# Row-maximum transposes ahead of the projections, and the low parts of Q and K taken by VectorE from PSUM

## The chip, the core and the metric

The kernel runs on one core of a Trainium2 chip. A core has five engines with instruction streams of their own: TensorE (PE in the profile; PEld is its weight load), VectorE (DVE), ScalarE (ACT), GpSimdE (POOL) and SyncE (SP), which here issues every DMA. They meet through semaphores. Matmul results go to PSUM, eight banks of 128 x 512 f32 values; everything else lies in SBUF. The metric is the device time of one execution in microseconds (us), lower being better.

## What is computed

```python
x = L0_attn_x                                    # 16 x 256 x 256, f32
xn = layernorm(x)
# attention, 16 heads of 16, causal, per batch of 256 rows
qkv = (xn @ w_qkv).reshape(b, s, 3, 16, 16)
scores = einsum('bqhd,bkhd->bhqk', q / 4, k); scores = where(causal, scores, NEG)
att = einsum('bhqk,bkhd->bqhd', softmax(scores), v).reshape(b, s, 256) @ w_out
# feed-forward part in fp8
ffn = (gelu(xn8 @ w_gating[0]) * (xn8 @ w_gating[1])) @ w_linear
out = x + att + ffn
```

## The kernel before, in words

The 4096 rows are worked off twice. First come 8 **chunks** of 512 rows: layer norm, transposes, the feed-forward part (gate L705, up L712, down L732), and the residual sum; the transposed normalised rows go to DRAM, split in a rounded high part and a low part. Behind chunk 5 the projections of batch 0 are made, behind chunk 6 the Q and K of batch 1 (`first_batches`).

Then 19 **steps** s = 0 to 18 pipeline the attention of the 16 batches (B = 16; `has(b)` is 0 <= b < 16). Heads are split in two halves c = 0, 1, and the score work of a half in two parts ii = 0, 1. A score call (`scores`, lines L771 to L829) does two jobs together: the maxima pass (mask matmuls L771, scores L792 and L825) of one half and the exponent pass (L809, L829) of an older one. In a full step PE runs, in this order,

- S1: maxima (s,0,0) with exponents (s-2,1,1); then QK: `project_qk` of batch s+1, L744, 12 matmuls to each of the banks `misc[0]` and `misc[1]`;
- S2: maxima (s,0,1) with exponents (s-1,0,0); then TM: two small transposes L857 of the row maxima of (s-1,1); then TV: probabilities times V of (s-2,1), L848;
- S3: maxima (s,1,0) with exponents (s-1,0,1); then V: `project_v` of batch s+1, L751; then OUT: `project_out` of batch s-3, L865;
- S4: maxima (s,1,1) with exponents (s-1,1,0); then TM of (s,0) and TV of (s-1,0).

QK, V, OUT, TM and TV all write one of the two banks of `misc`, and each waits for the reader of what stood there. S1 to S4 use the other six banks.

What the other engines do for it:

- DVE reduces each score result to row maxima (L497 for two banks, L500 for the third); a score call waits at its start for the L497 of the call before it (`max_done`). It also turns each TV result to rows (L507), divides it by the sum (L513, L515), and turns it back (L522).
- ACT copies Q and K out of `misc` twice: L593 rounds to the high part (`qk_part`), L596 copies them raw (`qk_raw`, in `w_raw`). POOL then subtracts (L353): low part = raw - high part. ACT also takes the exponents (L619, L621), negates the transposed maxima (`negate_max`, L610), and copies V (L604), the output (L636) and the attention rows (L630).
- POOL masks the exponents (L368, L372), splits the attention rows (L377) and adds x (L382).
- SP sends the parts of Q and K to the operand `stack` of the scores (`fill_stack`, L240, six DMAs for a batch) and the negated maxima to one row of it (`place_max`, L245). The exponent pass of a half waits for that row (`neg_in`). `place_max(s-1, 1)` stands behind the six DMAs of `fill_stack(s+1)` in SP's queue.

Nothing but this written order and the waits sets when something runs; all engines work in order.

## Time and profile before

| what | value |
|---|---|
| median of 3 runs | 385.46 us (385.41 to 386.12) |
| the profiled execution's own time | 386.55 us |
| its span, first to last instruction | 384.5 us |
| mean granted TensorE clock | 0.983 |
| busy: PE, DVE, ACT, POOL | 354.4 us (92%), 264.0 us (69%), 237.9 us (62%), 198.5 us (52%) |
| DMA | 57.5 MB moved, mean 150 GB/s |

A row of the timeline gives start, duration, engine, line, operation, output and inputs, and a count when like instructions are merged; square brackets hold how long the engine had been idle and who ended that. PE's matmuls overlap, so the time that a group takes is the distance from its start to the start of the next group, not its printed duration. The same goes for DVE and ACT, where the next instruction starts up to 0.1 us before the printed end of the last.

### The profile page before, as it was taken

To read this page: it belongs to the slowest core of one execution; us is meant where nothing else is said; L and a number is where in the kernel's file an instruction comes from. 1 tells how busy PE (TensorE), PEld (TensorE's weight loads), DVE (VectorE), ACT (ScalarE), POOL (GpSimd) and SP (SyncE) were. 2 spreads that over 40 slices of the span, in tenths; PEclk is the share of its full clock that TensorE was granted. 3 is DMA by queue.
4 is the path that set the end of the run, shared out by engine and by line. 5 is a ranking of instruction groups with operands and counts; after the bars stand their busy time and mean duration, and the time that the engine had idled before them with its cause. 6 is when DMAs were issued, how large, how long until landed. Compare 5 with 4: busy or idle time off the path is not lost.

```text
span 384.5 us, 9837 instructions
## 1 busy us (share of the span) xinstructions
PE 354.4 (92%) x3882; PEld 269.8 (70%) x3882; DVE 264.0 (69%) x444; ACT 237.9 (62%) x416; POOL 198.5 (52%) x268
## 2 busy tenths in 40 slices
PE   6698899998999889999999999999999999999882
PEld 6354465447475777778877888888888878886662
DVE  5768788885615565767767777776777677768741
ACT  0885666765664155676676666666757666666761
POOL 2351541234241134576666666865766657656773
PEclk9999999999999799999999999999999999999996
DMA  7985734930718034516436346255274362340001
GB/s 239 352 286 163 221 113 126 243 122 0 263 67 274 0 115 164 192 64 217 150 102 235 111 154 220 90 191 178 75 249 150 101 222 100 124 167 32 31 29 55
DMA packets 45453, 57.52 MB, mean 150 GB/s; under 512 B 2656, under 2 KB 36960, under 8 KB 45408
## 3 DMA queue, kind: packets, MB, share of 16 engines
q1 hardware_dynamic: 45408, 56.90, 45.3%
q8 instruction: 31, 0.51, 0.6%
q14 instruction: 14, 0.11, 0.1%
HBM read 16.78 MB, written 12.58 MB: 76 GB/s over the span
## 4 chain that ended last, share of the span: by engine, by line
PE 69%; DVE 8%; SPq 6%; ACT 5%; POOL 4%; issue 4%; DMA 4%; POOLq 0%; DVEq 0%; ACTq 0%
PE ps L744 11%; PE ps L848 10%; PE ps L732 7%; SPq L240 6%; PE ps L751 5%; PE ps L809 5%; PE ps L865 5%; PE ps L792 5%; PE ps L771 5%; PE ps L712 4%; PE ps L705 4%; DVE act L472 4%; PE ps L825 4%; DMA stack<-neg_max 3%; PE ps L681 2%
## 5 line engine op out<-in xcount | busy, mean ns | idle before, releaser
L497 DVE TENSOR_REDUCE row_max<-ps 128x8 f32<-128x1024 f32 x64 | 78.2, 1222 | 40.1 <-PE ps L792 40.0
L619 ACT ACTIVATE arena<-ps 128x1024 f32<-128x1024 f32 x64 | 65.8, 1028 | 43.2 <-PE ps L809 42.8
L368 POOL TENSOR_SCALAR_AFFINE_SELECT arena<-arena 128x1024 f32<-128x1024 f32 x64 | 55.5, 867 | 37.7 <-ACT arena L619 37.0
L472 DVE TENSOR_TENSOR act<-ps,gate 128x512 fp8e4<-128x512 f32 x64 | 43.1, 686 | 26.2 <-ACT gate L562 18.0
L353 POOL TENSOR_TENSOR qk_part<-w_raw,qk_part 128x512 fp32r<-128x512 f32 x32 | 41.0, 1281 | 33.3 <-ACT w_raw L596 32.4
L744 PE MATMUL ps<-xs,wq_part 128*128 128x256 f32 x384 | 50.2, 286 | 1.4 <-DVE wq_part L463 0.7
L744 PEld LDWEIGHTS ps<-xs,wq_part 128*128 128x128 f32 x384 | 46.9, 188 | 3.8 <-DVE wq_part L463 1.0
L848 PE MATMUL ps<-arena,v_aug 128*32 128x256 f32 (+1 forms) x1024 | 48.2, 329 | 0.6 <-POOL arena L372 0.5
L562 ACT ACTIVATE gate<-ps 128x512 bf16<-128x512 f32 x64 | 37.9, 599 | 17.1 <-PE ps L705 11.0
L500 DVE TENSOR_REDUCE row_max<-ps 128x2 f32<-128x512 f32 x64 | 43.5, 680 | 2.6 <-PE ps L825 2.6
L507 DVE STREAM_TRANSPOSE xn<-ps 128x512 f32<-128x512 f32 x32 | 22.9, 716 | 31.1 <-PE ps L848 31.1
L771 PE MATMUL ps<-above,pick 64*128 64x128 bf16 (+1 forms) x384 | 40.4, 242 | 2.6 <-DVE row_max L497 2.5
L712 PE MATMUL ps<-x,wg 128*128 128x512 fp8e4 x128 | 38.0, 378 | 4.9 <-DVE act L472 4.6
L848 PEld LDWEIGHTS ps<-arena,v_aug 128*32 128x32 f32 x1024 | 28.9, 109 | 18.3 <-issue 7.3
L705 PE MATMUL ps<-x,wg 128*128 128x512 fp8e4 x128 | 38.0, 379 | 2.1 <-ACT gate L562 1.0
L621 ACT ACTIVATE arena<-ps 128x512 f32<-128x512 f32 x64 | 38.3, 598 | 0.0
L809 PE MATMUL ps<-stack 64*128 64x128 f32 (+1 forms) x384 | 33.6, 280 | 4.2 <-DMA stack<-neg_max 2.9
L792 PE MATMUL ps<-stack 63*128 63x128 f32 (+1 forms) x384 | 36.7, 297 | 0.0
L382 POOL TENSOR_TENSOR w_raw<-w_raw,xres 128x512 f32<-128x512 f32 x16 | 20.4, 1273 | 28.9 <-ACT w_raw L636 28.9
L303 POOL TENSOR_SCALAR var_eps<-mean_var 128x4 f32<-128x4 f32 x8 | 2.1, 264 | 58.9 <-DVE mean_var L421 58.9
L809 PEld LDWEIGHTS ps<-stack 64*128 64x128 f32 x384 | 26.7, 187 | 6.5 <-DMA stack<-neg_max 4.7
L825 PE MATMUL ps<-stack 63*128 63x256 f32 x128 | 31.2, 324 | 0.0
(64 smaller groups left out, 626.1 us busy)
## 6 DMA issues: line engine op xcount, KB each, us to landing
stack<-qk_part SPq DMA_DIRECT2D x96, 256.0 KB, 2.9
xt_store<-xt_part SPq DMA_DIRECT2D x16, 512.0 KB, 4.1
xs<-xt_store SPq DMA_DIRECT2D x16, 512.0 KB, 3.9
out_dram<-w_raw SPq DMA_DIRECT2D x16, 256.0 KB, 2.2
xres<-in_L_attn_x_dram SPq DMA_DIRECT2D x7, 512.0 KB, 6.5
arena<-in_L_ffn_w_gating_dram SPq DMA_DIRECT2D x2, 1024.0 KB, 9.0
stack<-spare SPq DMA_DIRECT2D x4, 512.0 KB, 7.1
arena<-in_L_ffn_w_linear_dram SPq DMA_DIRECT2D x1, 1024.0 KB, 13.2
```

What stands on the lines that cost most here:

```text
L368: nc.gpsimd.affine_select(diag, diag, pattern=[[0, 1024 // width], [1, P]], compare_op=ALU.is_ge, fill=0.0, base=0, channel_multiplier=-1) ...
L472: nc.vector.tensor_tensor(act8[:, j, :], up_ps[j % 2][:], gate[:, j % 2, :], ALU.mult, saturate=False).then_inc(act_done, 1)
L497: nc.vector.tensor_reduce(to[:, :, 4 - heads:4], max_ps[:, 0:2, :].rearrange("p e (h k) -> p e h k", k=width), axis=AXIS_X, op=ALU.max).th ...
L619: nc.scalar.activation(arena[:, 3 * c + 2 * ii, :, :], exp_ps[:, 0:2, :], ACT.Exp).then_inc(exp_done, 1)
L705: last = nc.tensor.matmul(gate_ps[j % 2][:], wg8[:, 0, k, j * P:(j + 1) * P], x8[:, k, :], start=(k == 0), stop=(k == KD - 1))
L712: last = nc.tensor.matmul(up_ps[j % 2][:], wg8[:, 1, k, j * P:(j + 1) * P], x8[:, k, :], start=(k == 0), stop=(k == KD - 1))
L744: last = nc.tensor.matmul(misc[:, u, s * S:(s + 1) * S], wq_part[:, a, kt, col:col + P], xs[b % 2][:, z, kt, :], start=(i == 0), stop=(i = ...
L771: nc.tensor.matmul(max_ps[:, bank, :].rearrange("p (h k) -> p h k", k=width)[:, :, first:first + 64], pick[rows, i, :], above[rows, :].uns ...
L792: last = nc.tensor.matmul(max_ps[:, u, i * width:(i + 1) * width], st[rows, 4 * c + 4 - heads + i, 0, ii * P:(ii + 1) * P], st[rows, 4 * c ...
L809: last = nc.tensor.matmul(exp_ps[:, u, i * width:(i + 1) * width], est[rows, 4 * ec + 4 - heads + i, 1, kt * P:(kt + 1) * P], est[rows, 4 ...
L825: last_max = nc.tensor.matmul(max_ps[:, 2, cols], st[rows, 4 * c + i, 0, P:S], st[rows, 4 * c + i, 1, :], start=False, stop=(i == 1), skip ...
L848: last = nc.tensor.matmul(pv_bank(b, c)[32 * i:32 * i + 32, u * S + kt * P:(u + 1) * S], va[:, kt, 2 * (HG * c + i) + u, :], cols, start=( ...
```

## The change

Four things are edited.

- ACT's raw copy (L596), `qk_raw` and POOL's subtraction (L353) are gone. DVE subtracts the high part from the PSUM bank itself, in `split_qk`, which now stands in DVE's order between `normalize_o(s-2, 0)` and `find_max(s, 0, 1)`. Whoever waited for the raw copy (`qk_copied`) waits for this subtraction (`qk_lo`).
- TM of (s-1,1) moves from behind S2 to in front of QK, TM of (s,0) from the end of the step to directly behind S3. Both now write bank 1 of `misc`. The second half of QK (bank 1) waits for the first negation, V (bank 1) for the second.
- OUT now stands in front of V. TV of half 0 writes bank 0 instead of bank 1, except for the last half of all, (15,1), which has bank 1.
- ACT negates in the new order, ahead of the copies of Q and K and behind the exponents of S3; SP's `place_max` calls stand ahead of `fill_stack` and right behind it.

```diff
-            return misc[:, 1 if c == 0 or b == B - 1 else 0, :]
+            return misc[:, 1 if 2 * b + c == 2 * B - 1 else 0, :]
...
 (SP)
-                if s == B:
+                if has(s - 1):
                     place_max(s - 1, 1)
                 if s >= 1 and has(s + 1):
                     fill_stack(s + 1, 0)
                     fill_stack(s + 1, 1)
-                if has(s - 1) and s < B:
-                    place_max(s - 1, 1)
+                if has(s):
+                    place_max(s, 0)
                 if has(s + 3):
                     load_xs(s + 3)
                 if has(s - 3):
                     store_y(s - 3)
-                if has(s):
-                    place_max(s, 0)
...
 (DVE)
+            def split_qk(b, g):
+                dve.wait_ge(qk_hi[g], b + 1)
+                nc.vector.tensor_tensor(qk_part[:, g, QLO:KLO + 1:3, :], misc[:, g, :].rearrange("p (a s) -> p a s", a=2),
+                                        qk_part[:, g, QHI:KLO, :].bitcast(F32), ALU.subtract).then_inc(qk_lo[g], 1)
...
                 if has(s - 2):
                     normalize_o(s - 2, 0)
+                if s >= 1 and has(s + 1):
+                    split_qk(s + 1, 0)
+                    split_qk(s + 1, 1)
                 if has(s):
                     find_max(s, 0, 1)
...
 (ACT)
                 if has(s - 2):
                     exponent(s - 2, 1, 1)
+                if has(s - 1):
+                    negate_max(s - 1, 1)
                 if s >= 1 and has(s + 1):
                     copy_qk(s + 1, 0)
                     copy_qk(s + 1, 1)
...
                     exponent(s - 1, 0, 1)
+                if has(s):
+                    negate_max(s, 0)
+                if has(s - 3):
+                    copy_y(s - 3)
                 if has(s + 1):
                     evacuate_v(s + 1)
...
 (PE)
+                if has(s - 1):
+                    pe.wait_ge(*((v_done, s + 1) if has(s) else (neg_done[0], s)))
+                    transpose_max(s - 1, 1)
                 if s >= 1 and has(s + 1):
-                    pe.wait_ge(neg_done[0], s)
+                    pe.wait_ge(*((o_by_q_done, turned(s - 2, 0)) if s >= 2 else (ffn_done, 2 * CHUNKS)))
                     project_qk(s + 1, 0)
-                    pe.wait_ge(*((o_by_q_done, turned(s - 2, 0)) if s >= 2 else (v_done, 2)))
+                    pe.wait_ge(neg_done[1], s)
                     project_qk(s + 1, 1)
...
                 if has(s - 2) and s <= B:
-                    pe.wait_ge(*((qk_copied[0], s + 2) if has(s + 1) else (neg_done[0], s)))
+                    pe.wait_ge(*((qk_lo[0], s + 2) if has(s + 1) else (o_by_q_done, turned(s - 2, 0))))
                     times_v(s - 2, 1)
...
+                if has(s):
+                    pe.wait_ge(*((ffn_done, 2 * CHUNKS) if s == 0 else (qk_lo[1], s + 2) if has(s + 1) else (neg_done[1], s)))
+                    transpose_max(s, 0)
                 if has(s - 3):
...
                     for c in range(2):
                         project_out(s - 3, c)
+                if has(s + 1):
+                    pe.wait_ge(neg_done[0], s + 1)
+                    project_v(s + 1)
```

Where the order changes, a full step in the middle. **PE, S1 and the projections**, before and after (the first row is the last matmul of S1, the last three begin S2):

```order
L829 MATMUL ps<-stack 128x256
L744 MATMUL ps<-xs,wq_part 128x256 x24
L771 MATMUL ps<-above,pick 128x2x64 x4
L792 MATMUL ps<-stack 128x256 x4
L809 MATMUL ps<-stack 128x128 x8
```

```order
L818 MATMUL ps<-stack 128x256
L846 MATMUL ps<-ident,row_max 8x128 x2
L733 MATMUL ps<-xs,wq_part 128x256 x24
L760 MATMUL ps<-above,pick 128x2x64 x4
L781 MATMUL ps<-stack 128x256 x4
```

The two transposes (L857, now L846) stand in front of the projections (L744, now L733).

**DVE, first half of a step**, before and after, with the semaphores that each row waits for; L507/L499 turns the TV result, L497/L489 and L500/L492 are the maxima:

```order
L522 STREAM_TRANSPOSE xn<-o_norm 128x256 [waits ot_lo,o_norm_done]
L497 TENSOR_REDUCE row_max<-ps 128x2x2 [waits max_ready]
L500 TENSOR_REDUCE row_max<-ps 128x2 [waits max_ready]
L507 STREAM_TRANSPOSE xn<-ps 128x512 [waits pv_ready]
L497 TENSOR_REDUCE row_max<-ps 128x8 [waits max_ready]
```

```order
L514 STREAM_TRANSPOSE xn<-o_norm 128x256 [waits ot_lo,o_norm_done]
L472 TENSOR_TENSOR qk_part<-ps,qk_part 128x2x256 [waits qk_hi0]
L472 TENSOR_TENSOR qk_part<-ps,qk_part 128x2x256 [waits qk_hi1]
L489 TENSOR_REDUCE row_max<-ps 128x2x2 [waits max_ready]
L492 TENSOR_REDUCE row_max<-ps 128x2 [waits max_ready]
L499 STREAM_TRANSPOSE xn<-ps 128x512 [waits pv_ready]
```

The maxima of S2 are now queued behind the two subtractions.

**SP, one step**, before and after; L240/L238 fills the stack, L245/L243 places the maxima, L230/L228 loads `xs`, L250/L248 stores the output:

```order
L240 DMA stack1<-qk_part 32x4x512 [waits exp_ready,qk_lo0]
L240 DMA stack1<-qk_part 32x8x256 x2
L240 DMA stack1<-qk_part 32x4x512 [waits exp_ready,qk_lo1]
L240 DMA stack1<-qk_part 32x8x256 x2
L245 DMA stack3<-neg_max1 2x4x256 [waits neg_done1]
L230 DMA xs1<-xt_store 128x1024 [waits v_ready]
L250 DMA out_0_dram<-w_raw 128x2x256 [waits y_done]
L245 DMA stack0<-neg_max0 2x4x256 [waits neg_done0]
```

```order
L243 DMA stack3<-neg_max1 2x4x256 [waits neg_done1]
L238 DMA stack1<-qk_part 32x4x512 [waits exp_ready,qk_lo0]
L238 DMA stack1<-qk_part 32x8x256 x2
L238 DMA stack1<-qk_part 32x4x512 [waits exp_ready,qk_lo1]
L238 DMA stack1<-qk_part 32x8x256 x2
L243 DMA stack0<-neg_max0 2x4x256 [waits neg_done0]
L228 DMA xs0<-xt_store 128x1024 [waits v_ready]
L248 DMA out_0_dram<-w_raw 128x2x256 [waits y_done]
```

The maxima of half 1 are sent ahead of the six DMAs, those of half 0 ahead of the load and the store.

## Rows read from the trace of the kernel before

**Rows 1.** Timeline of PE, one step without a wait: start us, us, engine, line, what.

```profile
165.18 0.39 PE L771 MATMUL ps<-above,pick 64*128 64x256 bf16 x4
...
166.61 3.14 PE L744 MATMUL ps<-xs,wq_part 128*128 128x256 f32 x24
169.68 0.29 PE L771 MATMUL ps<-above,pick 64*128 64x128 bf16 x4
...
171.00 0.38 PE L857 MATMUL ps<-ident,row_max 128*8 128x128 f32 x2
171.31 1.51 PE L848 MATMUL ps<-arena,v_aug 128*32 128x256 f32 x32
172.75 0.39 PE L771 MATMUL ps<-above,pick 64*128 64x256 bf16 x4
...
174.18 1.68 PE L751 MATMUL ps<-wq_part,xs 128*128 128x256 f32 x12
175.69 1.60 PE L865 MATMUL ps<-wq_part,xt_part 128*128 128x256 f32 x12
177.22 0.28 PE L771 MATMUL ps<-above,pick 64*128 64x128 bf16 x4
...
180.30 0.39 PE L771 MATMUL ps<-above,pick 64*128 64x256 bf16 x4
```

**Rows 2.** Timeline of PE: S1 of step 15.

```profile
348.90 0.39 PE L771 MATMUL ps<-above,pick 64*128 64x256 bf16 x4
```

**Rows 3.** Waits of the whole span: total us, times, longest us.

```profile
PE ps L809 <- DMA stack<-neg_max: 2.9, 5, 0.8
```

**Rows 4.** Chain that ended last, step 14: start us, us, what.

```profile
343.84 0.04 issue
343.89 2.21 DMA stack<-neg_max
```

**Rows 5.** Timeline of ACT in the step of rows 1.

```profile
169.78 0.59 ACT L593 CAST qk_part<-ps 128x512 fp32r<-128x512 f32 x1 [0.36 <-PE ps L744]
...
179.64 0.36 ACT L610 ACTIVATE neg_max<-ps 8x256 fp32r<-8x256 f32 x1
```

**Rows 6.** Timeline of DVE: a subtraction from PSUM (chunk 7), a maximum (step 3).

```profile
107.38 1.29 DVE L439 TENSOR_TENSOR xt_part<-ps,xt_part 128x512 fp32r<-128x512 f32 x2 [1.97 <-ACT xt_part L553]
...
170.30 1.23 DVE L497 TENSOR_REDUCE row_max<-ps 128x4 f32<-128x1024 f32 x1 [1.15 <-PE ps L792]
```

**Rows 7.** Timeline of PE, chunk 7 and steps 0 and 1.

```profile
115.84 0.59 PE L712 MATMUL ps<-x,wg 128*128 128x512 fp8e4 x2 [0.23 <-DVE act L472]
...
128.80 0.61 PE L771 MATMUL ps<-above,pick 64*128 64x256 bf16 x4 [0.73 <-DVE row_max L497]
...
130.85 2.93 PE L751 MATMUL ps<-wq_part,xs 128*128 128x256 f32 x12
133.71 0.40 PE L771 MATMUL ps<-above,pick 64*128 64x128 bf16 x4
...
135.96 0.39 PE L771 MATMUL ps<-above,pick 64*128 64x256 bf16 x4
...
137.10 3.14 PE L744 MATMUL ps<-xs,wq_part 128*128 128x256 f32 x24
...
143.74 0.51 PE L809 MATMUL ps<-stack 64*128 64x256 f32 x4 [0.88 <-ACT arena L619]
...
147.70 0.66 PE L809 MATMUL ps<-stack 64*128 64x128 f32 x8 [0.84 <-DMA stack<-neg_max]
```

**Rows 8.** Busy time by stretch: us, PE, PEld, DVE, ACT, POOL, granted clock, DMA.

```profile
125.40:128.80 3.40, 1.74 (x21) 1.13 (x20) 3.10 (x4) 0.07 (x1) 1.15 (x1) 1.00 0.00 0
128.80:135.70 6.90, 6.90 (x42) 5.81 (x42) 3.38 (x4) 0.58 (x1) 0.00 (x0) 0.51 0.11 29
```

**Rows 9.** Timeline of the last steps: one row of ACT, one of PE.

```profile
357.23 0.59 ACT L636 COPY w_raw<-ps 128x512 f32<-128x512 f32 x1 [0.51 <-PE ps L865]
...
363.35 1.51 PE L848 MATMUL ps<-arena,v_aug 128*32 128x256 f32 x32 [0.52 <-POOL arena L372]
```

More of the change, by code:

```diff
@@ L128, in attention_ffn @@
         max_ready, max_done = sem("max_ready"), sem("max_done")
-        qk_copied = [sem(f"qk_copied{i}") for i in range(2)]
         maxt_ready = [sem(f"maxt_ready{i}") for i in range(2)]
@@ L348, in _ @@
             make_masks()
-            def split_qk(b, g):
-                pool.wait_ge(qk_hi[g], b + 1)
-                pool.wait_ge(qk_copied[g], b + 1)
-                nc.gpsimd.tensor_tensor(qk_part[:, g, QLO:KLO + 1:3, :], qk_raw[:, g, :, :], qk_part[:, g, QHI:KLO, :].bitcast(F32),
-                                        ALU.subtract).then_inc(qk_lo[g], 1)
-            def first_batches(b):
-                for g in range(2):
-                    split_qk(b, g)
-            ffn_steps(step, first_batches)
+            ffn_steps(step, no_projection)
             def mask(b, c, ii):
@@ L386, in _ @@
                     mask(s - 2, 1, 1)
-                if s >= 1 and has(s + 1):
-                    split_qk(s + 1, 0)
-                    split_qk(s + 1, 1)
                 if has(s - 1):
@@ L485, in step, with first_batches @@
                     split_wq(c - 2)
-            ffn_steps(step, no_projection)
+            def split_qk(b, g):
+                dve.wait_ge(qk_hi[g], b + 1)
+                nc.vector.tensor_tensor(qk_part[:, g, QLO:KLO + 1:3, :], misc[:, g, :].rearrange("p (a s) -> p a s", a=2),
+                                        qk_part[:, g, QHI:KLO, :].bitcast(F32), ALU.subtract).then_inc(qk_lo[g], 1)
+            def first_batches(b):
+                for g in range(2):
+                    split_qk(b, g)
+            ffn_steps(step, first_batches)
             def find_max(b, c, ii):
@@ L593, in copy_qk @@
                 nc.scalar.copy(qk_part[:, g, QHI:KLO, :], made).then_inc(qk_hi[g], 1)
-                if b >= 1:
-                    act.wait_ge(qk_lo[g], b)
-                nc.scalar.copy(qk_raw[:, g, :, :], made).then_inc(qk_copied[g], 1)
             def evacuate_v(b):
@@ L609, in negate_max @@
                     act.wait_ge(neg_in[c], 16 * b)
-                nc.scalar.mul(neg_max[c][:, :], misc[0:PAIRS, c, 0:S], -1.0).then_inc(neg_done[c], 1)
+                nc.scalar.mul(neg_max[c][:, :], misc[0:PAIRS, 1, 0:S], -1.0).then_inc(neg_done[c], 1)
             def exponent(b, c, ii):
@@ L651, in _ @@
                     copy_qk(s + 1, 1)
-                if s == B:
-                    negate_max(s - 1, 1)
                 if has(s - 1):
                     exponent(s - 1, 0, 0)
-                if has(s - 1) and s < B:
-                    negate_max(s - 1, 1)
-                if has(s - 1):
                     exponent(s - 1, 0, 1)
+                if has(s):
+                    negate_max(s, 0)
+                if has(s - 3):
+                    copy_y(s - 3)
                 if has(s + 1):
                     evacuate_v(s + 1)
-                if has(s - 3):
-                    copy_y(s - 3)
                 if has(s - 2):
@@ L667, in _ @@
                     exponent(s - 1, 1, 0)
-                if has(s):
-                    negate_max(s, 0)
                 if has(s - 2):
@@ L720, in step @@
                     if c >= CHUNKS - 2:
-                        pe.wait_ge(*((v_done, 1) if i == 0 and c == CHUNKS - 2 else (qk_copied[i], c - CHUNKS + 3)))
+                        pe.wait_ge(*((v_done, 1) if i == 0 and c == CHUNKS - 2 else (qk_lo[i], c - CHUNKS + 3)))
                     elif started:
@@ L912, in _ @@
                     scores((s, 1, 1) if has(s) else None, (s - 1, 1, 0) if has(s - 1) else None)
-                if has(s):
-                    pe.wait_ge(*((y_copied, s - 2) if s >= 3 else (o_by_q_done, 2) if s == 2 else
-                                 (qk_copied[0], 3) if s == 1 else (ffn_done, 2 * CHUNKS)))
-                    transpose_max(s, 0)
                 if has(s - 1):
-                    pe.wait_ge(*((v_done, s + 2) if has(s + 1) else (neg_done[1], s)))
+                    pe.wait_ge(*((y_copied, s - 2) if s >= 3 else (o_by_q_done, 2) if s == 2 else (qk_lo[0], 3)))
                     times_v(s - 1, 0)
```

19 lines of the change are left out of this document (5 added, 14 removed).

## The prediction

> **What bounds the kernel now.** I read the page's busy shares first (PE 92%), then the busy time by stretches, then PE's timeline. A step of the attention part without a wait takes 15.12 us, from one S1 to the next [rows 1], and in it PE has no idle time: S1 1.43, QK 3.07, S2 1.32, TM 0.31, TV 1.44, S3 1.43, V 1.51, OUT 1.53, then S4, TM and TV. So a change that leaves PE's matmuls alone, as this one does, can win nothing from fewer copies or from an idle GpSimd. It can only win PE's waits. Those are few. Steps 3 to 14 take 348.90 - 165.18 = 183.72 us [rows 1, 2], where 12 x 15.12 would be 181.44: **2.28 us are lost there**. The list of waits names what for: PE waits five times, 2.9 us, for the negated maxima of half 1 [rows 3], two of the five in steps 1 and 2, the rest in this stretch. The chain shows why they are late: the DMA of 2.21 us [rows 4] is issued behind the six DMAs of Q and K, which wait for POOL's subtraction. The other places with idle PE are the first steps, where the pipeline is not yet full [rows 7], and the end [rows 9].
>
> **Part 1, the maxima's DMA (gain 2.28).** TM of (s-1,1) now runs at S1 + 1.43. ACT negates behind the exponents of S1. In the old S4 the same sequence (exponents, then L610) ends at 179.64 + 0.36 = 180.00, 2.78 us behind its S4 at 177.22 [rows 1, 5]; take 2.9 for a call that begins with S1's larger mask. The DMA is then under way at S1 + 3.5 and lands near 5.7; S4 wants it at about S1 + 12.7. The maxima of half 0 also leave earlier than before and are wanted a step later. All waits of rows 3 go, in full: 2.28 us in steps 3 to 14; those of steps 1 and 2 are in part 4.
>
> **Part 2, new waits of a full step (0, but thin).** Four places.
> - QK bank 1 waits for the negation, S1 + 2.9; PE gets there at 1.43 + 0.31 + 1.44 = 3.18. Fits by 0.25.
> - V waits for the second negation, S3 + 2.9; PE gets there at S3 + 1.43 + 0.31 + 1.53 = 3.27, thanks to OUT in front. Fits by 0.35.
> - QK bank 0 and OUT wait for L507 of DVE; they fit by about 0.9 and 0.5.
> - S3 waits for the maximum L497 of S2, and this now stands behind the two subtractions. Walk it from S2 = 169.68: ACT's copy of bank 1 starts at 169.78 and ends at 170.37 [rows 5]. A hand-over between engines is 0.04 us in the chain [rows 4], so DVE starts the subtraction at 170.40. Its price is not in the attention part, but the same form (128x512, PSUM minus SBUF) is L439: two take 1.29 us, one 0.68 with 0.61 to the next start [rows 6]. So L497 starts at 171.01, where it started at 170.30, and ends 1.23 later at 172.24; with a hand-over PE can go on at 172.29. PE reaches S3 at 169.68 + 1.32 + 1.44 = 172.44, as TM no longer lies between. **It fits by 0.15 us.** I take 0; the other end is in the rivals.
>
> The raw copies free 2 x 0.48 us of ACT and the subtractions 2 x 1.28 us of POOL in a step; neither is waited for by PE in a full step, so this is worth 0. What is left is the order itself. TM's 0.31 us is more than two matmuls at QK's spacing (3.07 / 24 = 0.13), so some 0.18 of it is a changeover to TV; every group of rows 1 has one where it meets another kind. The change leaves the number of these meetings as it is, so I count 0, between -0.1 and +0.1 a step, 1.2 us either way.
>
> **Part 3, the end of the feed-forward part (gain 0.3).** In chunk 7 the third up matmul waits 0.23 us for DVE [rows 7], which waits for ACT, which makes the raw copy (0.48) first. Without it I get 115.36 for 115.84, a gain of 0.48. In chunk 6 V of batch 0 now waits for DVE's subtraction, a loss of 0.2. S1 of step 0 comes 0.3 earlier.
>
> **Part 4, steps 0 to 2 (loss 1.2).** There is no OUT before step 3 and no TV behind S2 before step 2, so nothing covers the new waits.
> - Step 0. S3 starts at 128.5 for 128.80 and TM follows it. V waits for a TM, a negation (0.36) and two hand-overs: 0.56 us of wait. V takes 2.86 and S4 1.63 [rows 7] up to 135.94. S1 of step 1 then waits for the maximum of S4, which TM used to cover: 0.62. It starts at 136.56 for 135.96, **+0.60**.
> - Step 1. S1 1.13, TM, QK 3.07, S2 1.33. With no TV, S3 waits for the queue of part 2: 2.62 - 1.33 = 1.29. The first exponents still hold S3 up a little (0.13; it was 0.88 [rows 7]). V waits for the negation behind TM, some 1.1. S4 needs no DMA any more (0.84 [rows 7]). With V 1.63, S4 1.33 and TV 1.44 the step is 14.63, before 14.50: **+0.13**.
> - Step 2. V waits 2.9 + 0.05 - 1.74 = 1.2; the DMA wait, worth 1.0, goes: **+0.17**.
> S1 of step 3 comes at 166.08 for 165.18: with part 3's 0.3 inside, +0.90.
>
> **Part 5, the end (loss 0.25).** In steps 15 and 16 QK and V are over. TM (0.31) now stands in front of OUT, so ACT's L636 comes at S1 + 8.58, before 357.23 - 348.90 = 8.33 [rows 2, 9]. POOL adds x behind it and masks after that, and TV waits for the mask (363.35, [rows 9]). This chain runs to the end, so 0.25 is lost.
>
> **Sum.** +0.90 - 2.28 + 0.25 = **-1.13 us** on a span of 384.5, so 383.4. The profiled execution took 386.55, 1.1 more than the median of the runs; I apply the difference to the median: 385.46 - 1.13 = **384.3 us**. A measurement of this kernel tells about 0.2%, 0.8 us, from no change: below 384.7 is faster, above 386.2 slower.
>
> **Rivals.**
> - *The clock falls again (slower).* In 125.4 to 128.8 PE was busy 1.74 of 3.4 us, with scores that wait for maxima; behind it the granted clock was 0.51, the 1.2 GHz level, for 6.9 us of full work [rows 8]. V took 2.86 us there where a full step has 1.51 [rows 7, 1]. The new step 1 looks alike: from 142.4 to 146.8 PE would wait 1.29, 0.13 and 1.1 us, busy for 1.9 of 4.4 us. For it: these figures. Against it: this S3 holds exponents too, and the old step 1 with its waits of 0.88 and 0.84 [rows 7] did not bring the clock down. Price: S3, V and S4 of the old slow stretch took 2.05 + 2.86 + 1.63 for some 1.4 + 1.6 + 1.1, so 2.4, up to 3.4 for 6.9 us of half rate. Time 384.3 + 2.9 = 387.2. It decides if the new step 1 is as thin as the stretch ahead of the fall. Chance 0.25. The Trainium skill, "TensorE: Matmul & The Clock Gate", section "What's actually happening", has the slow rate as the default that activity lifts; the trace agrees, since it fell behind the thin stretch of rows 8.
> - *S3 waits in each step (slower).* If the subtraction or its hand-overs cost over 0.15 us more than L439's, all 12 steps pay the rest. With 0.3 us more it is 12 x 0.15 = 1.8, with 0.4 it is 3.0: 386.1 to 387.3. For: the margin; DVE's queue takes no other order. Against: L439 keeps its time and ACT is idle before that copy, 0.36 us [rows 5]. Chance 0.12, at 386.7.
> - *More is won (faster).* The slow clock of step 0 may not come, or be shorter, as S1 to S3 start 0.3 earlier; or QK behind TM starts without the slow first pair. 1.5 to 2.8 us: near 382.3. Chance 0.12.
> - *The new meetings cost more (slower).* If TM to TV were cheap today and TM to QK, TM to OUT and scores to TV each cost a changeover of their own, a step would have two more of some 0.1 us beyond the usual spacing: 12 x 0.2 = 2.4, 386.7. Against: TM to TV shows the 0.18 already [rows 1]. Chance 0.05. The Trainium skill, "TensorEngine Tiling (Array Packing)", has the rule that would make it so: a change of the tiling mode drains the array; TM is a narrow tile like TV, and the projections are not.
> - *It does nothing where it should.* The waits for the maxima go, but another wait of the same size takes their place in steps 3 to 14 (TV for the masks, OUT for L507). Then parts 3 to 5 are left, 0.90 + 0.25 above today: 386.6. Against: the margins of part 2. Chance 0.04.
>
> **The numbers.** The forecast keeps 0.42; its own range is 383.0 to 385.5, by the order term and the start. Some 0.30 of it lies below 384.7, the rest within the limits. With the 0.12 of "more is won", faster has 0.42. The clock (0.25) is slower as a whole; of the other 0.21, 0.07 stays within the limits. So same has 0.19 and slower 0.39. For 8 in 10 the range must take in the clock's case and half of "more is won": **382.6 to 387.5**.
>
> **What would show it.** L809 no longer waits for neg_max; steps 3 to 14 take 15.1 each. L497 behind the subtractions ends within 2.6 us of S2, and S3 shows no idle time for DVE in steps 3 to 14 (wrong if it does: then 0.15 was not there). In steps 0 to 2 PE waits for L610 in front of V, 0.6, 1.1 and 1.2 us. One slow stretch of the clock: a second one, near 146 to 153, is the first rival. The end from S1 of step 15 is 0.25 longer.

## The result and the profile after

| | before | after |
|---|---|---|
| median | 385.44 us (4 runs, 383.27 to 386.12) | 380.12 us (4 runs, 378.96 to 382.02) |
| ratio of the times | | 0.986, 95% interval 0.981 to 0.991 |
| span of the profiled execution | 384.5 us | 377.2 us |
| start to S1 of step 0 | 124.78 us | 124.66 us |
| steps 0 to 2 | 40.40 us | 39.66 us |
| steps 3 to 14 | 183.72 us | 176.52 us |
| S1 of step 15 to the end | 35.56 us | 36.39 us |

The change made the kernel faster by 5.3 us, 1.4%. The forecast was 384.3 us, in a range from 382.6 to 387.5: the direction was right, the gain was several times larger, and the measured time lies below the range. The span fell by 7.2 us, and the steps 3 to 14 alone fell by 7.2 us; the rest gives and takes back about as much. The medians differ by less than the two spans because the profiled execution before (386.55 us) lay 1.1 us above its median, and the one after (378.96 us) 1.2 us below.

Here and below the medians take in every execution, and the ratios leave out those that were slowed, among them one of 435.7 us of the changed kernel when it was run again and one of 485.1 us of the kernel with idle matmuls.

The same view as [rows 1], PE's timeline, for step 3 of the kernel after. The group lines are L760 (masks, the start of a score call), L846 (TM), L733 (QK), L837 (TV), L854 (OUT), L740 (V); L814 is the last matmul of a score call. The last row is S1 of step 15, the partner of [rows 2]:

```profile
164.32 0.39 PE L760 MATMUL ps<-above,pick 64*128 64x256 bf16 x4
...
165.54 0.28 PE L814 MATMUL ps<-stack 63*128 63x256 f32 x1
165.75 0.38 PE L846 MATMUL ps<-ident,row_max 128*8 128x128 f32 x2
165.88 3.11 PE L733 MATMUL ps<-xs,wq_part 128*128 128x256 f32 x24
168.93 0.28 PE L760 MATMUL ps<-above,pick 64*128 64x128 bf16 x4
...
170.04 0.28 PE L814 MATMUL ps<-stack 63*128 63x256 f32 x1
170.25 1.51 PE L837 MATMUL ps<-arena,v_aug 128*32 128x256 f32 x32
171.69 0.39 PE L760 MATMUL ps<-above,pick 64*128 64x256 bf16 x4
...
173.11 0.38 PE L846 MATMUL ps<-ident,row_max 128*8 128x128 f32 x2
173.25 1.68 PE L854 MATMUL ps<-wq_part,xt_part 128*128 128x256 f32 x12
174.77 1.57 PE L740 MATMUL ps<-wq_part,xs 128*128 128x256 f32 x12
176.27 0.29 PE L760 MATMUL ps<-above,pick 64*128 64x128 bf16 x4
...
177.60 1.51 PE L837 MATMUL ps<-arena,v_aug 128*32 128x256 f32 x32
179.04 0.39 PE L760 MATMUL ps<-above,pick 64*128 64x256 bf16 x4
...
340.85 0.39 PE L760 MATMUL ps<-above,pick 64*128 64x256 bf16 x4
```

A full step takes 179.04 - 164.32 = 14.72 us, where it took 15.12, and now every one of the twelve does: (340.85 - 164.32) / 12 = 14.71. Read the distances from start to start. Most groups are as before: S2 1.32, TV 1.44, S3 1.42, OUT 1.52, V 1.50. QK is 3.05 for 3.07. What differs is TM: it takes 0.13 in front of QK and 0.14 in front of OUT. In [rows 1], in front of TV, the same two transposes took 0.31. They are the same work with the same printed duration of 0.38.

PE's waits in the kernel after (total us, times, longest): the line of [rows 3] has no successor, and two others stand there that concern the change.

```profile
PE ps L760 <- DVE row_max L489: 4.2, 6, 1.2
...
PE ps L740 <- ACT neg_max L602: 2.7, 3, 1.1
```

PE's timeline again: the third up matmul of chunk 7, and the waits of steps 0 and 1 (answers to [rows 7]); the time in brackets is the idle time ahead of the row.

```profile
115.72 0.59 PE L701 MATMUL ps<-x,wg 128*128 128x512 fp8e4 x2
...
128.68 0.39 PE L760 MATMUL ps<-above,pick 64*128 64x256 bf16 x4 [0.73 <-DVE row_max L489]
...
130.82 2.79 PE L740 MATMUL ps<-wq_part,xs 128*128 128x256 f32 x12 [0.46 <-ACT neg_max L602]
...
135.44 0.39 PE L760 MATMUL ps<-above,pick 64*128 64x256 bf16 x4 [0.90 <-DVE row_max L489]
...
142.36 0.39 PE L760 MATMUL ps<-above,pick 64*128 64x256 bf16 x4 [1.21 <-DVE row_max L489]
...
145.28 1.68 PE L740 MATMUL ps<-wq_part,xs 128*128 128x256 f32 x12 [1.12 <-ACT neg_max L602]
```

DVE's timeline in step 3, the answer to [rows 6] (L472 is the new subtraction, L489 the maximum of S2):

```profile
169.65 0.69 DVE L472 TENSOR_TENSOR qk_part<-ps,qk_part 128x512 fp32r<-128x512 f32 x1 [0.74 <-ACT qk_part L588]
170.26 1.22 DVE L489 TENSOR_REDUCE row_max<-ps 128x4 f32<-128x1024 f32 x1
```

Busy time by stretch in the kernel after (us, then PE, PEld, DVE, ACT, POOL, granted clock, DMA), the answer to [rows 8]:

```profile
129.90:133.30 3.40, 2.94 (x13) 2.49 (x13) 1.44 (x2) 0.37 (x1) 0.00 (x0) 0.50 0.01 2
...
351.80:355.20 3.40, 2.08 (x26) 1.37 (x18) 2.02 (x4) 2.81 (x5) 3.40 (x6) 1.00 0.23 77
355.20:358.60 3.40, 3.23 (x36) 2.09 (x37) 0.38 (x1) 0.63 (x2) 1.48 (x3) 0.50 0.01 2
```

The granted clock of the first steps fell to 0.50, the 1.2 GHz level, 1.1 us later than in [rows 8] and for 3.4 us instead of 6.9. A new slow stretch came in step 16, behind 3.4 us in which PE was busy 2.08 us.

### The profile page after: what moved, and what is told of

It is laid out like the page before. It is cut to its first block, busy times and chain, and to the rows that moved or that the text cites. A ratio compares the mean times of both kernels' runs of the same rounds, so it can differ in the third digit from the quotient of the medians.

```text
span 377.2 us, 9773 instructions
## 1 busy us (share of the span) xinstructions
PE 346.9 (92%) x3882; PEld 268.7 (71%) x3882; DVE 280.4 (74%) x476; ACT 224.4 (59%) x384; POOL 158.9 (42%) x236
## 4 chain that ended last, share of the span: by engine, by line
PE 79%; DVE 9%; ACT 5%; issue 3%; POOL 2%; DMA 1%; POOLq 0%; DVEq 0%; ACTq 0%
PE ps L733 12%; PE ps L837 11%; PE ps L721 7%; PE ps L740 7%; PE ps L854 6%; PE ps L781 6%; PE ps L760 6%; PE ps L798 5%; PE ps L694 5%; PE ps L701 4%; PE ps L814 4%; DVE act L455 4%; PE ps L846 2%; PE ps L670 2%; DVE row_max L489 2%
## 5 line engine op out<-in xcount | busy, mean ns | idle before, releaser
L489 DVE TENSOR_REDUCE row_max<-ps 128x8 f32<-128x1024 f32 x64 | 77.6, 1213 | 26.1 <-PE ps L781 26.0
L733 PE MATMUL ps<-xs,wq_part 128*128 128x256 f32 x384 | 49.8, 285 | 1.4 <-DVE wq_part L446 0.7
L837 PE MATMUL ps<-arena,v_aug 128*32 128x256 f32 (+1 forms) x1024 | 49.5, 335 | 0.9 <-POOL arena L358 0.8
L733 PEld LDWEIGHTS ps<-xs,wq_part 128*128 128x128 f32 x384 | 47.0, 189 | 2.2 <-DVE wq_part L446 1.0
L760 PE MATMUL ps<-above,pick 64*128 64x128 bf16 (+1 forms) x384 | 39.8, 239 | 4.3 <-DVE row_max L489 4.2
L492 DVE TENSOR_REDUCE row_max<-ps 128x2 f32<-128x512 f32 x64 | 43.5, 679 | 0.0
L837 PEld LDWEIGHTS ps<-arena,v_aug 128*32 128x32 f32 x1024 | 29.5, 111 | 16.7 <-issue 2.0
L472 DVE TENSOR_TENSOR qk_part<-ps,qk_part 128x512 fp32r<-128x512 f32 x32 | 22.1, 692 | 19.9 <-ACT qk_part L588 19.9
L499 DVE STREAM_TRANSPOSE xn<-ps 128x512 f32<-128x512 f32 x32 | 22.8, 712 | 16.5 <-PE ps L837 16.5
L588 ACT CAST qk_part<-ps 128x512 fp32r<-128x512 f32 x32 | 18.8, 587 | 23.4 <-PE ps L733 23.4
L854 PE MATMUL ps<-wq_part,xt_part 128*128 128x256 f32 x192 | 27.3, 291 | 3.6 <-POOL xt_part L363 3.6
L814 PE MATMUL ps<-stack 63*128 63x256 f32 x128 | 30.6, 319 | 0.0
L721 PE MATMUL ps<-wl,act 128*128 128x256 fp8e4 x256 | 29.4, 273 | 0.3 <-issue 0.3
```

The source lines that it names most:

```text
L489: nc.vector.tensor_reduce(to[:, :, 4 - heads:4], max_ps[:, 0:2, :].rearrange("p e (h k) -> p e h k", k=width), axis=AXIS_X, op=ALU.max).th ...
L721: last = nc.tensor.matmul(down_ps[i][:, t * D:(t + 1) * D], act8[:, j, tok:tok + P], wl8[:, j, :], start=(j == 0), stop=(j == J - 1))
L733: last = nc.tensor.matmul(misc[:, u, s * S:(s + 1) * S], wq_part[:, a, kt, col:col + P], xs[b % 2][:, z, kt, :], start=(i == 0), stop=(i = ...
L760: nc.tensor.matmul(max_ps[:, bank, :].rearrange("p (h k) -> p h k", k=width)[:, :, first:first + 64], pick[rows, i, :], above[rows, :].uns ...
L837: last = nc.tensor.matmul(pv_bank(b, c)[32 * i:32 * i + 32, u * S + kt * P:(u + 1) * S], va[:, kt, 2 * (HG * c + i) + u, :], cols, start=( ...
```

## Experiments

Ratios are against the kernel before on the same chip: the first four kernels below ran on one chip, the next four (up to the first run of V first) on a second, the last four on a third. The steps 3 to 14 are free of slow clock in every profile, so they are compared directly; the first and last steps are not.

### One half of the change at a time

The changed kernel again, as the partner of the next three:

> The changed kernel again, beside the next three on the same chip. Theory A (a TM in front of 128-wide matmuls has no changeover behind it, which wins 0.4 us in each of 12 full steps): 379 to 382 us, full steps of 14.72 us. How long the slow stretches of the clock are is open: 3.4 us each in the first profile, and the spread of the runs (379.0 to 382.0) may come from them.

Measured: 381.6 us, ratio 0.986 (0.979 to 0.993). Steps 3 to 14 took 176.52 us again, to the hundredth.

**The subtraction alone.** The order of the kernel before stays.

```diff
-                nc.scalar.copy(qk_raw[:, g, :, :], made).then_inc(qk_copied[g], 1)
...
+                dve.wait_ge(qk_hi[g], b + 1)
+                nc.vector.tensor_tensor(qk_part[:, g, QLO:KLO + 1:3, :], misc[:, g, :].rearrange("p (a s) -> p a s", a=2),
+                                        qk_part[:, g, QHI:KLO, :].bitcast(F32), ALU.subtract).then_inc(qk_lo[g], 1)
...
-                    pe.wait_ge(*((qk_copied[1], s + 2) if has(s + 1) else (o_by_q_done, turned(s - 2, 0))))
+                    pe.wait_ge(*((qk_lo[1], s + 2) if has(s + 1) else (o_by_q_done, turned(s - 2, 0))))
                     transpose_max(s - 1, 1)
```

> The kernel before with only the subtraction moved to VectorE (raw copies and GpSimd's subtraction gone); order of the transposes and banks as before. Theory A: TM still stands in front of TV, so a full step keeps at least 15.12 us; TM behind S2 now waits for the subtraction of bank 1, 0.1 to 0.2 us a step; the waits for the maxima's DMA go. 384 to 386 us. Rival B (the gain comes from the freed ScalarE and GpSimd and the earlier low parts, wherever TM stands): full steps of 14.7, 380 to 381 us.

Measured: 383.2 us, ratio 0.992 (0.988 to 0.996), a little faster than the 384 to 386 expected, far from the rival's 380 to 381. Steps 3 to 14 took 183.21 us, a full step 15.27. PE's timeline of step 3 in this kernel (L765 begins S2, L851 is TM, L842 TV):

```profile
167.45 0.28 PE L765 MATMUL ps<-above,pick 64*128 64x128 bf16 x4
...
168.92 0.38 PE L851 MATMUL ps<-ident,row_max 128*8 128x128 f32 x2
169.23 1.51 PE L842 MATMUL ps<-arena,v_aug 128*32 128x256 f32 x32
```

From S2 to TM it is 1.47 us, where [rows 1] have 1.32: TM writes the bank from which DVE still subtracts, and waits 0.15 for it in each step. The six DMAs leave earlier, since POOL's subtractions are gone, so the waits of [rows 3] go too, 2.28 us; 12 x 0.15 = 1.8 of them are lost again. TM to TV is 0.31 as before. The rest of its gain lies in steps 0 to 2 (38.29 us for 40.40) and in the end (34.91 for 35.56); most of the latter is the clock, which in the kernel before was slow during the last OUT (378.0 us on) and here only behind it.

**The order alone.** The raw copies and POOL's subtractions stay, PE, ACT and SP have the new order, and TV of half 0 the new bank.

```diff
+                if has(s - 1):
+                    pe.wait_ge(*((v_done, s + 1) if has(s) else (neg_done[0], s)))
+                    transpose_max(s - 1, 1)
                 if s >= 1 and has(s + 1):
...
                     project_qk(s + 1, 0)
...
-                if has(s - 1) and s < B:
-                    pe.wait_ge(*((qk_copied[1], s + 2) if has(s + 1) else (o_by_q_done, turned(s - 2, 0))))
-                    transpose_max(s - 1, 1)
```

> The changed kernel with ScalarE's raw copies and GpSimd's subtraction brought back: only the order, the banks and the place of the maxima in SP's queue are changed. Theory A: full steps of 14.72 us and no wait for the maxima, since place_max now stands ahead of the six DMAs: 379.5 to 381.5 us, 0.5 more at most than the changed kernel. Rival B: 384 us or more.

Measured: 384.4 us, ratio 0.996 (0.992 to 1.000). The 379.5 to 381.5 us expected were missed, and as a whole this kernel is hardly faster than the one before. Yet steps 3 to 14 took **176.52 us, all of the 7.2 us of the whole change**. So in the steady part the gain belongs to the order, none of it to the subtraction. But steps 0 to 2 took 45.40 us, for 39.66 in the changed kernel. Busy time by stretch of this kernel:

```profile
130.00:143.70 13.70, 12.69 (x71) 10.99 (x70) 5.46 (x6) 2.40 (x5) 0.33 (x1) 0.50 0.12 41
147.10:150.50 3.40, 1.66 (x15) 1.16 (x16) 1.77 (x2) 2.88 (x5) 2.46 (x4) 1.00 1.00 341
150.50:153.90 3.40, 3.40 (x26) 3.18 (x26) 0.21 (x1) 0.58 (x1) 0.00 (x0) 0.50 0.03 11
```

The slow clock lasted 13.7 us and came back at 150.5, in the stretch that the first rival named. Its ten executions have a mean clock of 0.962 to 0.977, those with the subtraction alone 0.980 to 0.993. Why the slow stretch lasts longer here isn't settled.

**Idle matmuls in step 0.** Behind S1 and S2 of step 0 PE makes 8 and 6 matmuls whose results nobody reads.

```diff
+            def busy(n, bank):
+                for i in range(n):
+                    nc.tensor.matmul(ps[:, bank, 0:2 * P], pick[:, 0, :], pick[:, :, :].rearrange("p i q -> p (i q)"), start=True, stop=True)
...
+                if s == 0:
+                    busy(8, 0)
```

> The changed kernel with 8 and 6 idle 256-column bf16 matmuls of PE put in the two waits for maxima of step 0 (0.9 and 0.7 us idle). Theory C (the slow stretch of the clock follows the idle time of step 0): no slow stretch near 130 us, step 0 shorter by 1 to 1.5 us, the runs 1 to 2 us faster than the changed kernel's on the same chip. Rival D (the idle time is not what brings it, or the slow stretch costs nothing since DVE's waits take its place): the same time within 0.5 us.

Measured: 380.0 us, ratio 0.981 (0.972 to 0.990); three of its four executions took 377.0, 377.9 and 382.0 us with a mean clock of 0.999, 0.994 and 0.976. The profile is of the last. Busy time by stretch:

```profile
125.30:128.80 3.50, 3.48 (x36) 2.43 (x36) 3.17 (x4) 0.11 (x1) 1.15 (x1) 1.00 0.00 0
...
140.00:143.40 3.40, 1.80 (x24) 1.32 (x24) 3.11 (x4) 3.18 (x5) 1.50 (x3) 1.00 1.04 354
143.40:153.60 10.20, 9.52 (x82) 7.68 (x83) 3.21 (x5) 2.72 (x5) 2.41 (x4) 0.50 0.24 83
```

With PE busy in 125.3 to 128.8 the clock did not fall in step 0. It fell instead behind the thin stretch of step 1, where S3 waits 1.2 us. So what the first rival describes does happen; whether it strikes differs from one execution to the next. Step 0 took 9.52 us for 10.78, but the expected 1 to 2 us of the whole time are not shown: the intervals of this ratio and of the changed kernel's overlap. Nothing else moved: steps 3 to 14 took 176.52 us.

### What the place of TM is worth

The next two put a second, useless pair of the same transposes into the changed kernel, into bank 0, whose next user overwrites it.

```diff
                                  (o_by_q_done, turned(s - 2, 0)) if s == B + 1 else (y_copied, s - 3)))
+                    if has(s + 1):
+                        for t in range(QT):
+                            nc.tensor.transpose(misc[0:PAIRS, 0, t * P:(t + 1) * P], row_max[:, s % 2, t, 0:PAIRS], ident[:])
                     for c in range(2):
                         project_out(s - 3, c)
```

> The changed kernel with a second pair of the small transposes (TM) in steps 3 to 14, right behind the pair of S3, in front of OUT; its result is overwritten. Read from the profile: steps 3 to 14 take 176.5 us without it. Theory A (TM costs only its two matmuls, 0.11 us each, where it stands next to another TM and to 128-wide work): 12 x 0.22 more, 179.1. Rival (each TM brings its changeovers along): 12 x 0.3 or more, 180.1 or above.

The other one has the same two transposes between S4 and TV:

```diff
                     pe.wait_ge(*((y_copied, s - 2) if s >= 3 else (o_by_q_done, 2) if s == 2 else (qk_lo[0], 3)))
+                    if s >= 3 and has(s + 1):
+                        for t in range(QT):
+                            nc.tensor.transpose(misc[0:PAIRS, 0, t * P:(t + 1) * P], row_max[:, s % 2, t, 0:PAIRS], ident[:])
                     times_v(s - 1, 0)
```

> The same second pair of transposes, but between S4 and TV. Theory A (TM in front of TV has a changeover of 0.2 us behind it and one in front, where there was one): 12 x 0.31 more, steps 3 to 14 in 180.2 us; the start of TM to the start of TV 0.31, where TM to QK has 0.14. Rival by tile modes (TM is a narrow tile like TV, so TM to TV is free and TM to wide work is not): 0.2 or less a step, 178.9 or below.

Measured, in one execution of each: steps 3 to 14 took 179.08 us with the pair next to OUT, 180.31 with the pair next to TV; 179.1 and 180.2 were expected. That is 0.21 and 0.32 us a step for the same two instructions. PE's timelines, first of the one, then of the other:

```profile
174.37 0.38 PE L846 MATMUL ps<-ident,row_max 128*8 128x128 f32 x2
174.59 0.38 PE L893 MATMUL ps<-ident,row_max 128*8 128x128 f32 x2
174.72 1.55 PE L854 MATMUL ps<-wq_part,xt_part 128*128 128x256 f32 x11
```

```profile
179.05 0.38 PE L908 MATMUL ps<-ident,row_max 128*8 128x128 f32 x2
179.36 1.51 PE L837 MATMUL ps<-arena,v_aug 128*32 128x256 f32 x32
```

The pair in front of OUT ends its turn after 0.13 us, the pair in front of TV after 0.31. A pair behind another pair makes the first one take 0.22 for 0.14; that too is a price, and it hides nearly half of the difference in the sums. The rival of the second run, that TM goes free with TV as a narrow tile and pays beside wide ones, is refuted: it asked for 178.9 us or less.

### How thin S3 is

DVE subtracts bank 1 twice; the first result goes to a spare tile.

```diff
+            def split_again(b):
+                dve.wait_ge(qk_hi[1], b + 1)
+                nc.vector.tensor_tensor(again[:, :].rearrange("p (a s) -> p a s", a=2), misc[:, 1, :].rearrange("p (a s) -> p a s", a=2),
+                                        qk_part[:, 1, QHI:KLO, :].bitcast(F32), ALU.subtract)
...
                     split_qk(s + 1, 0)
+                    split_again(s + 1)
                     split_qk(s + 1, 1)
```

> The changed kernel with one more subtraction of the same form on VectorE (into a spare tile) ahead of the one for bank 1, in every step. Theory of the 0.15 us margin: the maximum of S2 comes 0.61 later, S3 waits 0.46 us in each full step, steps 3 to 14 take 176.5 + 5.5 = 182.0 us. Rival (VectorE has more room than worked out): under 1 us more. Rival (it has none): 0.61 a step, 183.8.

Measured, in one execution: steps 3 to 14 took 181.70 us (182.0 expected), 5.18 more, 0.43 a step. DVE's and PE's timelines of one step (L484 is the added subtraction, L495 the maximum, L767 the masks of S3):

```profile
180.00 0.69 DVE L484 TENSOR_TENSOR again<-ps,qk_part 128x512 f32<-128x512 f32 x1 [0.74 <-ACT qk_part L595]
180.60 0.68 DVE L473 TENSOR_TENSOR qk_part<-ps,qk_part 128x512 fp32r<-128x512 f32 x1
181.20 1.21 DVE L495 TENSOR_REDUCE row_max<-ps 128x4 f32<-128x1024 f32 x1
```

```profile
182.47 0.39 PE L767 MATMUL ps<-above,pick 64*128 64x256 bf16 x4 [0.37 <-DVE row_max L495]
```

The added instruction moved L495 by 0.60, and 0.43 arrived at PE: the margin of S3 is 0.17 us. The prediction had walked it to 0.15.

### Better first steps

In steps 0 to 2 V waits for a negation. Since TM and V write the same bank, and V does not need TM, V can go first there.

```diff
+                if s < 3:
+                    pe.wait_ge(*((ffn_done, 2 * CHUNKS) if s == 0 else (qk_lo[1], s + 2)))
+                    project_v(s + 1)
...
                     scores((s, 1, 1) if has(s) else None, (s - 1, 1, 0) if has(s - 1) else None)
+                if s < 3:
+                    pe.wait_ge(v_done, s + 2)
+                    transpose_max(s, 0)
```

> The changed kernel with, in steps 0 to 2 alone, V directly behind S3 and TM behind S4, in front of TV, as it was before the change. Theory (V waits there only for the negation of a TM that stands in front of it): the waits of 0.46, 1.1 and 1.1 us for L602 go, 0.31 - 0.14 comes back a step, so S1 of step 0 to S1 of step 3 takes 37.5 to 38.3 us instead of 39.7, if the clock does the same; 1 to 2 us off the time. With less idle time in step 1 the clock is less likely to fall there.

Measured: 375.9 us, ratio 0.975 (0.968 to 0.982), the four executions from 373.4 to 379.1. That is more than the 1 to 2 us expected; the profile kept the full clock in the first steps. It was run again on another chip, beside three versions that build on it:

> The early-step variant again (V ahead of TM in steps 0 to 2), beside the next three on the same chip: 373.4 us where the clock never falls in the first steps, 377 to 379 where it does; median near 376, spread of 3 us or more.

Measured: 377.0 us, ratio 0.974 (0.969 to 0.980), six executions from 373.3 to 380.9. The two profiles of this one kernel differ by 4.0 us, and show what the clock costs. Steps 0 to 2 took 35.20 us in the first, which kept the full clock there, and 37.73 in the second; the end took 35.11 and 36.29. Stretches of the second (the one of the start):

```profile
122.10:128.90 6.80, 5.30 (x55) 4.11 (x53) 2.94 (x3) 1.17 (x2) 2.30 (x2) 1.00 0.11 36
128.90:135.70 6.80, 6.63 (x41) 5.80 (x42) 3.28 (x5) 0.58 (x1) 0.00 (x0) 0.50 0.00 0
```

So 6.8 us at the slow clock cost 2.5 us in the start, and a stretch of 3.4 us in the end costs 1.2. The first of the two kept the full clock although nothing filled PE's waits in step 0, so one profile with idle matmuls, as above, does not show that they hold the clock; a set of executions can.

**With the idle matmuls of step 0** added:

> The early-step variant with PE kept busy in the two waits for maxima of step 0 (8 and 6 idle 256-column matmuls). Theory C (the slow stretches follow PE's idle time, and between them the idle time of steps 0 and 1 makes the spread): without the thin stretch of step 0 and with only the wait of step 1 left, no slow stretch ahead of the last steps in most runs: steps 0 to 2 in 35.2 us, 373 to 375 us, spread under 2 us. Rival D (phase alone decides, whatever PE does there): median and spread as in the variant without them, near 376.

Measured: 374.6 us, ratio 0.970 (0.966 to 0.974). All six executions lie between 373.7 and 375.0, a spread of 1.3 us where the same kernel without the idle matmuls has 7.6, or 4.1 without its slowest execution.

**With the maximum of S2 ahead of the subtractions in step 1**, where nothing covers the queue, and with ACT's table of exponents loaded in step 0, ahead of the first exponents:

```diff
+                if s == 1:
+                    find_max(s, 0, 1)
                 if s >= 1 and has(s + 1):
                     split_qk(s + 1, 0)
                     split_qk(s + 1, 1)
-                if has(s):
+                if has(s) and s != 1:
                     find_max(s, 0, 1)
...
+            nc.scalar.activation(exp_once[:], ident[:], ACT.Exp)
```

> As the last, and in step 1 alone the maximum of S2 stands ahead of VectorE's two subtractions, and ScalarE loads the table of the exponential in step 0. Theory: S3 of step 1 waited 1.2 us for that maximum; it waits 0.5 now, and the exponents no longer wait for the table: 0.7 to 1.2 us off, 372 to 374 us. Rival: another wait takes its place, no gain.

Measured: 373.7 us, ratio **0.968 (0.964 to 0.972), the fastest kernel here** by its median, though the interval overlaps with the last one's; six executions from 372.6 to 374.3. PE's waits of step 1 and ACT's table load in its profile:

```profile
140.82 0.39 PE L767 MATMUL ps<-above,pick 64*128 64x256 bf16 x4 [0.51 <-DVE row_max L490]
...
142.61 1.69 PE L747 MATMUL ps<-wq_part,xs 128*128 128x256 f32 x12 [0.30 <-DVE qk_part L473]
```

```profile
126.64 1.28 ACT L641 ACT_TABLE_LOAD   x1
```

S3 waits 0.51 for 1.21, V waits 0.30 for the subtractions that now come later: 0.4 us is the net, and steps 0 to 2 took 34.86 us for 35.18. In the version before, the table load of 1.28 us ran at 138.50, directly ahead of the first exponents, and no wait of PE there was for ACT; what moving it is worth by itself was not run.

### An attempt at the end

In the last steps POOL adds x (L369, 1.27 us) ahead of masks. I put it behind, in step 17 between the two splits.

```diff
-                if has(s - 3):
+                if has(s - 3) and s < B - 1:
                     add_x(s - 3)
...
+                if has(s - 3) and s >= B - 1 and s != B + 1:
+                    add_x(s - 3)
```

> As the last, and in steps 15 to 18 GpSimd adds x behind its masks and splits instead of ahead of them. Theory (the end hangs on GpSimd's queue: add, mask, split, then TV and OUT): the waits of 0.8 us of TV and 1.25 us of OUT for GpSimd shrink, S1 of step 15 to the end takes 33 to 34 us instead of 35.1: 371 to 373 us. Rival: the last store waits for the adds instead, no gain.

Measured: 377.5 us, ratio 0.977 (0.973 to 0.982), 3.8 us worse than without. From S1 of step 15 to the end it took 39.87 us for 34.98. POOL's timeline and PE's, around S4 and TV of step 16 in this kernel:

```profile
346.33 1.09 POOL L355 TENSOR_SCALAR_AFFINE_SELECT arena<-arena 128x1024 f32<-128x1024 f32 x1 [2.06 <-ACT arena L619]
...
349.31 1.26 POOL L369 TENSOR_TENSOR w_raw<-w_raw,xres 128x512 f32<-128x512 f32 x1
350.53 0.63 POOL L355 TENSOR_SCALAR_AFFINE_SELECT arena<-arena 128x512 f32<-128x512 f32 x1
```

```profile
351.67 2.79 PE L849 MATMUL ps<-arena,v_aug 128*32 128x256 f32 x32 [2.05 <-POOL arena L359]
```

The addition used to fill POOL's idle time ahead of the exponents; POOL now idles 2.06 us there and does it in front of the mask for which TV waits: 2.05 for 0.83. The same happens once more at TV of step 17 (1.31 us). A slow stretch of 6.8 us from 350.8 on, behind these waits, adds to it: TV takes 2.71 us to the next start for 1.44. "Behind the masks" of one call was ahead of the masks of the next.

## Why the prediction fell short

Its sum took 1.13 us off the span; 7.23 went. The 6.1 us between them:

| step of the prediction | predicted | measured | difference |
|---|---|---|---|
| part 1, the maxima's DMA, steps 3 to 14 | -2.28 | -2.28 | 0 |
| part 2, new waits of a full step | 0 | 0 | 0 |
| part 2, the order itself, steps 3 to 14 | 0 (1.2 either way) | -4.92 | **-4.92** |
| part 3, end of the feed-forward part | -0.30 | -0.12 | +0.18 |
| part 4, steps 0 to 2 without part 3 | +1.20 | -0.74 | -1.94 |
| part 5, the end | +0.25 | +0.83 | +0.58 |

**The step that failed is the order term of part 2.** The prediction said that TM's changeover is one of many meetings of unlike groups and that the change leaves their number as it is, "so I count 0". Measured, the order is worth 4.92 us. In front of QK or OUT the two transposes cost 0.13 or 0.14 to the next start; in front of TV they cost 0.31. Twice a step that is 0.35, and QK behind TM is 0.02 and OUT and V together 0.02 shorter than before: 0.39 of the 0.41 that a step fell. The runs hold it up. With the order alone steps 3 to 14 take 176.52 us; with the subtraction alone TM to TV is still 0.31 and they take 183.21; and the doubled pairs differ by 0.10 us a step by their place. In the kernel with V first, TM stands in front of TV in steps 1 and 2 and takes 0.31 there, and 0.14 in front of QK in the same profile.

Single rows show which meetings cost. First the kernel before, the second transpose of TM and the first matmul of TV; then the kernel after, the second transpose and the first two matmuls of QK:

```profile
171.11 0.27 PE L857 MATMUL ps<-ident,row_max 128*8 128x128 f32 x1
171.31 0.40 PE L848 MATMUL ps<-arena,v_aug 128*32 128x256 f32 x1
```

```profile
165.85 0.27 PE L846 MATMUL ps<-ident,row_max 128*8 128x128 f32 x1
165.88 0.48 PE L733 MATMUL ps<-xs,wq_part 128*128 128x256 f32 x2
```

From TM to TV it is 0.20 us, from TM to QK 0.03, where transposes follow each other after 0.11. From the last matmul of a score call to the next group it is 0.21, whether that is TM (165.54 to 165.75) or TV (170.04 to 170.25). So the number of dear meetings did change: behind S2 there were two, scores to TM and TM to TV, and now there is one, scores to TV; behind S1 there was one, scores to QK, and there is one still, scores to TM.

The prediction's 0.18 for the changeover does not follow from its own figures: two matmuls at QK's spacing of 0.13 make 0.26 and leave 0.05 of the 0.31. That 0.18 lies near the measured 0.17 is luck. Its bound of 0.1 a step had no row behind it either. Had it kept its 0.18 as a price of these two neighbours, the upper end would have been 12 x 2 x 0.18 = 4.3 us, and 0 if the price follows TM everywhere. The direction came out right without this term: the other parts together took 2.3 us off, which by itself would have given 383.1 us (an estimate from the median before), inside the range.

The rival "QK behind TM starts without the slow first pair" had the sign, but its own mechanism is the small part: QK's second matmul starts 0.20 us behind the first, where it was 0.22. And it was put at 2.8 us at the most, together with a shorter slow clock.

The rival of **dearer meetings** had the wrong sign. It rested on the rule in the Trainium skill, "TensorEngine Tiling (Array Packing)", section "Key Properties", that a change of the tiling mode drains the array, and on counting TM as a narrow tile like TV. The second is what the rows contradict: TM goes over to QK without a gap and to TV with one. The kernel places TV's matmuls by name in 32-wide column tiles (`tile_position`), and TM's transposes not. Count TM, for all its 8 columns, with the 128*128 groups, and the rule fits these rows, with 0.20 to 0.21 us at the changes shown between 63*128, 128*8 or 128*128, and 128*32, and has the right sign for this edit. No run changes the tile of TM alone, so this is a reading that fits, not one that is shown.

**Part 1 held.** The line of [rows 3] is gone. Since every full step is now the same, nothing of the 2.28 us is left. The reading behind it was loose: only three of the five listed waits lie in steps 3 to 14, with 1.24 us of idle time. Each of these steps lasted 0.25 us longer than its idle time says, and a fourth one took 15.37 us without a wait in the list. The experiments add that either half of the change removes them: the new order sends the maxima ahead of the six DMAs, the subtraction lets the six leave earlier.

**Part 2's waits held to 0.02 us.** L489 starts at 170.26 and ends 1.22 later at 171.48; with a hand-over of 0.05 PE could start S3 at 171.53, and did at 171.69: 0.16 of margin for the 0.15 predicted. Doubling the subtraction gave 0.17. S3 waits in none of the steps 3 to 14. The raw copies and subtractions that went were worth nothing in a full step, as predicted. The other two margins are 0.2 us each, for 0.25 and 0.35: the negations end at 167.20 and 174.57, and PE comes to QK's second half at 167.40 and to V at 174.77, both sooner since TM is cheaper. (The prediction put half of QK at 1.44 us; half of 3.07 is 1.53.)

**Part 3.** V of batch 0 cost 0.37 us in chunk 6 where 0.2 was counted (the first gate matmul of chunk 7 comes at 113.48 for 113.11). The third up matmul came at 115.72, which gives back 0.12 in all, for 0.3. In nine other profiles of kernels alike up to there S1 of step 0 began between 124.56 and 125.06, so 0.12 is within what profiles differ by.

**Part 4** had its waits right and their cover wrong. V waited 0.46, 1.12 and 1.12 us (predicted 0.56, 1.1 and 1.2), S3 of step 1 waited 1.21 (1.29). But the sum for step 0 had S3, V and S4 at the slow clock of [rows 8]. The slow stretch began 1.1 us later and lasted 3.4 us, so S3 took 1.13 for 2.05 and S4 took 1.00 for 1.63; S1 of step 1 then waited 0.90 for 0.62. Step 0 was 10.78 us long for a predicted 12.08. That is luck of the execution: the kernels with a second pair of TM have the same steps 0 to 2, their slow stretch there lasted 6.8 us, and their step 0 took 11.87 and 12.17 us. Steps 1 and 2 were 0.42 and 0.22 shorter than predicted. TM in front of QK was 0.17 cheaper in each, and in step 1 the predicted 0.13 for the first exponents did not come.

**Part 5 and the clock rival.** Without any slow clock before the last OUT, the end takes 35.11 us in the new order and 34.91 with the subtraction alone: 0.2 for a predicted 0.25. The other 0.6 of the difference is the clock: a stretch of 3.4 us in step 16, worth 1.2 us, against one that in the kernel before fell on the last OUT. So the rival's mechanism did strike, in another place than the one named. In step 1 it spared the changed kernel's profile and struck with the order alone and with the idle matmuls.

## What to carry to other kernels

Price the meetings of unlike matmul groups one by one, from start to start in the timeline: a small group can cost more than twice as much in front of one neighbour (0.31 us here) as in front of another (0.13), and in a loop that is a gain without any change of work. If an edit changes who stands beside whom, the row with the extra time bounds the gain, and is not a detail. And when an instruction is moved out of a queue's busy stretch, look first whether it had been filling idle time there.
